# A new engine order, one semaphore per step, the attention product and the split maxima read from PSUM, and pair sums in a buffer of their own, in a fused attention and feed-forward kernel

## The reference

```python
def attention(q, k, v):                      # q = layernorm(x), k = v = ctx
    # (16, 256, 512) is read as 16 * 8 heads of (32, 512)
    qk = einsum('bdm,bdn->bmn', qh, kh) / sqrt(32)     # 512 x 512 scores per head
    return einsum('bmn,bcn->bcm', softmax(qk), vh)
def act_quant(x):                            # to 8 bit levels, one scale per token
    scale = 127 / clip(max(abs(x), axis=-1), 1e-5)
    return clip(round(x * scale), -128, 127) / scale
def weight_quant(w):                         # to -1, 0, 1, one scale for the matrix
    scale = 1 / clip(mean(abs(w)), 1e-5)
    return clip(round(w * scale), -1, 1) / scale
def bitlinear(x, w): return act_quant(x) @ weight_quant(w).T
x = x + attention(layernorm(x), ctx, ctx)
x = x + bitlinear(silu(bitlinear(layernorm(x), W1)), W2)   # W1 2048x512, W2 512x2048
```

## Time and profile before

| | |
|---|---|
| median of 3 executions | 919.39 us (917.77 to 921.04) |
| the profiled execution: its time, its span | 921.06 us, 919.0 us |
| busy PE, DVE | 791.9 us (86%), 789.7 us (86%) |
| busy ACT, POOL | 671.6 us (73%), 617.5 us (67%) |
| mean granted TensorE clock | 0.976 of full speed |

### The profile page before, as it was taken

The page is one execution under the profiler, slowest core; times in us unless marked ns, Lnnn a source line. Parts: engine busy times, 40 slices in busy tenths (PEclk is TensorE's granted clock), DMA queues, the critical chain, the costliest instruction groups (busy, mean ns, idle before and its releaser), DMA issues.

```text
span 919.0 us, 13936 instructions
## 1 busy us (share of the span) xinstructions
PE 791.9 (86%) x4580; PEld 292.9 (32%) x4580; DVE 789.7 (86%) x1624; ACT 671.6 (73%) x1089; POOL 617.5 (67%) x619
## 2 busy tenths in 40 slices
PE   1667799998999999999999999899999999989875
PEld 0322233333333333333333333333333333333222
DVE  1958799999999999999999999999999999998552
ACT  3485687877777777787777777787777778777753
POOL 4125578776777777777777777777777777875651
PEclk9977999999999999999999999999999999999997
DMA  8550333222333333312233333212233333120000
GB/s 264 156 158 18 70 81 70 61 63 63 71 81 81 82 81 70 82 47 65 63 81 81 82 81 81 70 50 67 60 79 81 81 82 81 47 58 25 24 12 23
DMA packets 49927, 68.28 MB, mean 74 GB/s; under 512 B 6336, under 2 KB 30912, under 8 KB 49344
## 3 DMA queue, kind: packets, MB, share of 16 engines
q1 hardware_dynamic: 49856, 67.39, 29.2%
HBM read 33.55 MB, written 8.39 MB: 46 GB/s over the span
## 4 chain that ended last, share of the span: by engine, by line
PE 51%; DVE 35%; issue 7%; POOL 3%; ACT 2%; DMA 1%; SPq 0%; POOLq 0%; ACTq 0%; DVEq 0%
PE bank_b L918 12%; DVE mx L703 11%; PE pv L887 9%; PE mxp L877 8%; PE st L867 7%; DVE hmx L782 6%; DVE late L777 6%; PE bank_b L956 4%; PE bank_a L956 3%; PE bank_a L908 3%; DVE cparts L713 2%; PE dn L898 1%; PE bank_a L926 1%; POOL late L492 1%; DVE sm L756 1%
## 5 line engine op out<-in xcount | busy, mean ns | idle before, releaser
L465 POOL TENSOR_TENSOR probs<-probs 128x512 f32<-128x512 f32 x256 | 332.8, 1317 | 138.5 <-PE pv L887 125.2
L703 DVE TENSOR_REDUCE mx<-mxp 128x1 f32<-128x512 f32 x512 | 338.1, 680 | 60.8 <-PE mxp L877 58.9
L546 ACT ACTIVATE probs<-st,sm 128x512 f32<-128x512 f32 x512 | 343.1, 686 | 53.0 <-PE st L867 49.8
L877 PE MATMUL mxp<-ks,qs 96*128 96x512 f16 x512 | 201.5, 395 | 56.8 <-DVE mx L703 24.9
L867 PE MATMUL st<-qs,ks 98*128 98x512 f16 x512 | 197.9, 388 | 5.3 <-DMA qs<-crow 3.1
L887 PE MATMUL pv<-probs,vt 128*32 128x512 f32 x1024 | 142.7, 630 | 0.0
L918 PE MATMUL bank_b<-w2t,late 128*128 128x512 f16 x512 | 134.7, 388 | 2.6 <-ACT late L578 2.6
L867 PEld LDWEIGHTS st<-qs,ks 98*128 98x128 f16 x512 | 50.1, 98 | 145.5 <-ACT probs L546 63.4
L877 PEld LDWEIGHTS mxp<-ks,qs 96*128 96x128 f16 x512 | 53.4, 105 | 132.1 <-DVE mx L703 65.2
L782 DVE TENSOR_REDUCE hmx<-late 128x1 f32<-128x512 f32 x128 | 84.6, 681 | 2.2
L609 ACT ACTIVATE late<-bank_a,sm 128x512 f32<-128x512 f32 x64 | 44.0, 688 | 50.4 <-PE bank_a L956 50.4
(11 more groups left out here) (92 smaller groups left out, 1024.9 us busy)
## 6 DMA issues: line engine op xcount, KB each, us to landing
xs<-x SPq DMA_DIRECT2D x32, 256.0 KB, 4.0
cs<-ctx SPq DMA_DIRECT2D x32, 256.0 KB, 4.1
ks<-kh SPq DMA_DIRECT2D x64, 128.0 KB, 3.4
qs<-qh SPq DMA_DIRECT2D x64, 128.0 KB, 3.7
xr<-x SPq DMA_DIRECT2D x32, 256.0 KB, 4.0
out<-late SPq DMA_DIRECT2D x32, 256.0 KB, 2.0
probs<-w SPq DMA_DIRECT2D x4, 1024.0 KB, 9.0
ks<-kl SPq DMA_DIRECT2D x32, 128.0 KB, 3.2
```

The costliest lines, as they stand in the source:

```text
L465: pool.tensor_tensor(probs[:, 2 * pair, h, :], probs[:, 2 * pair, h, :], probs[:, 2 * pair + 1, h, :], ALU.add).then_inc(sum_done, 1)
L546: act.activation(probs[:, c, h, :], st[u % 2][:, :], ACT.Exp, scale=sm1[:, r, ESC:ESC + 1]).then_inc(exp_done, 1)
L703: dve.reduce_max(mx[:, slot.ring(off), NC * h + c:NC * h + c + 1], mxp[m % 2][:, :], axis=AX.X).then_inc(max_done, 1)
L877: pe.matmul(mxp[m % 2][:, :], qs[0:3 * DH, r, h, c * P:(c + 1) * P], ks[0:3 * DH, r, h, :], start=True, stop=True).then_inc(mx_done, 1)
```

## The change

```diff
-    values=[6, 10, 15, 18],
-    sums=[6, 7, 8, 9, 14, 15, 16, 17],
-    denominators=[12, 19],
-    pv_evac=[18],
+    values=[16, 18, 19, 19],
+    sums=[2, 4, 5, 5, 7, 7, 7, 9],
+    denominators=[16, 18],
...
-    abs=[-18, -17, -16, -15, -2, -2, 2, 4],
-    ones=[-20],
-    sum=[-12, 5],
-    quantise=[-12, -11, -9, -9, 7, 9, 11, 15],
-    groups=[-10, -9, -7, -7, -6, -5, -4, -3, 9, 10, 12, 13, 15, 16, 18, 19],
+    abs=[-25, -23, -17, -16, -15, -9, -6, -2],
+    sum=[-14, 1],
+    quantise=[-14, -12, -11, -4, 2, 5, 9, 15],
+    groups=[-13, -12, -12, -7, -4, -3, -2, -1, 5, 8, 11, 13, 15, 17, 21, 23],
...
-                    wait_alone(pool, pv_done, slot, NC, off, 2 * pair + 1, passed)
+                    wait(pool, dn_done, slot, 2, off - 1, pair + 1)
                 wait(pool, exp_done, slot, UNITS, off, TH * (2 * pair + 1) + h + 1)
-                pool.tensor_tensor(probs[:, 2 * pair, h, :], probs[:, 2 * pair, h, :], probs[:, 2 * pair + 1, h, :],
+                pool.tensor_tensor(sums[:, pair, h, :], probs[:, 2 * pair, h, :], probs[:, 2 * pair + 1, h, :],
                                    ALU.add).then_inc(sum_done, 1)
...
-                if u % (2 * TH) == 0:
-
-                    wait(act, dn_done, slot, 2, -1, c // 2 + 1)
+                if h == 0:
+                    wait(act, pv_done, slot, NC, -1, c + 1)
+                wait(act, sum_done, slot, 2 * TH, -1, TH * (c // 2) + h + 1)
...
-                act.copy(pvs[:, slot.ring(off) % 2, :], pv[:, :]).then_inc(pv_evac, 1)
...
-                act.copy(crow[:, slot.ring(off) % 2, :], bank_a[0:2 * UNITS, 0:P // 2].bitcast(f16)).then_inc(ct_evac, 1)
+                act.copy(crow[:, slot.ring(off) % 2, 0, :], bank_a[0:UNITS, 0:P]).then_inc(ct_evac, 1)
...
+            dve.memset(ks[3 * DH:P, :, :, :], -1.0).then_inc(minus_ones, 1)
...
-                dve.tensor_copy(cparts[:, r, 0, :], mx[:, r, :]).then_inc(cpart_done, 1)
...
-                dve.tensor_tensor(cparts[:, r, 1, :], mx[:, r, :], cparts[:, r, 0, :], ALU.subtract).then_inc(cpart_done, 1)
+                dve.tensor_tensor(crow[:, k, 1, :], bank_a[0:UNITS, 0:P], crow[:, k, 0, :], ALU.subtract).then_inc(ct_low, 1)
...
-                dve.tensor_tensor(att[:, k, :], pvs[:, k, :], rden[:, :], ALU.mult).then_inc(token_scales, 1)
+                dve.tensor_tensor(att[:, k, :], pv[:, :], rden[:, :], ALU.mult).then_inc(attended, 1)
```

More of the change, by code:

```diff
@@ L50 @@
+    maxima=[-22, -21, -20, -20, -19, -18, -17, -15, -13, -12, -12, -10, -9, -9, -8, -7],
     vt=[-7],
-    vt_evac=[-7],
-    cparts=[-6],
+    vt_evac=[-8],
     ct=[-4],
     ct_evac=[-5],
-    values=[6, 10, 15, 18],
-    sums=[6, 7, 8, 9, 14, 15, 16, 17],
-    denominators=[12, 19],
-    pv_evac=[18],
-    invert=[20],
+    ct_low=[-4],
+    values=[16, 18, 19, 19],
+    sums=[2, 4, 5, 5, 7, 7, 7, 9],
+    denominators=[16, 18],
+    invert=[19],
     attend=[22],
-    residual=[23],
+    residual=[14],
@@ L82 @@
-    key_scale_b=[-28],
-    moments=[-32],
+    rstd2=[18],
+    xn2=[19],
+    absmax2=[25],
+    scale2=[25],
+    quantise=[20],
+    xqt=[27],
+    xqt_evac=[26],
+    first=[28, 29, 30, 31],
+    tanh=[28, 29, 31, 31],
+    gate=[28, 29, 32, 32],
+    hidden_max=[30, 32, 33, 34],
+    hidden_scale=[34],
+    hidden_quantise=[27, 28],
+    ht=[36, 39],
+    ht_evac=[36, 39],
+    second=[38, 39, 41, 42],
+    finish=[41],
+    max_read=[-21, -21, -21, -20, -19, -18, -16, -14, -11, -10, -10, -10, -8, -8, -7, -6],
@@ L103 @@
-    quantise=[-12, -11, -9, -9, 7, 9, 11, 15],
-    groups=[-10, -9, -7, -7, -6, -5, -4, -3, 9, 10, 12, 13, 15, 16, 18, 19],
-)
-ORDER = {'pool': ['key_rsqrt', 'xn', 'quantise', 'hidden_quantise', 'residual', 'ql', 'finish', 'rstd2', 'rstd',
-          'xn2', 'sums'],
- 'act': ['kh', 'vt_evac', 'tanh', 'ct_evac', 'qh', 'pv_evac', 'ht_evac', 'rescale', 'key_squares', 'xqt_evac',
-         'quantise_act'],
- 'dve': ['max_read', 'key_scale_b', 'cparts', 'norm2', 'cparts_low', 'aggregate', 'hidden_scale',
-         'hidden_scale_b', 'attend', 'hidden_scale_c', 'norm2b', 'absmax2', 'invert_b', 'key_scale',
-         'invert_c', 'invert', 'gate', 'hidden_max', 'moments2', 'hidden_scale_d', 'scale2', 'kl', 'scale2_b',
-         'moments', 'stats_x'],
- 'pe': ['xqt', 'key_norm', 'maxima', 'ct', 'values', 'vt', 'first', 'ht', 'second', 'denominators']}
+    abs=[-25, -23, -17, -16, -15, -9, -6, -2],
@@ new lines @@
+    sum=[-14, 1],
+    quantise=[-14, -12, -11, -4, 2, 5, 9, 15],
+    groups=[-13, -12, -12, -7, -4, -3, -2, -1, 5, 8, 11, 13, 15, 17, 21, 23],
+)
+ORDER = {'pool': ['residual', 'ql', 'sums', 'key_rsqrt', 'xn', 'xn2', 'hidden_quantise', 'rstd2', 'finish',
+          'quantise', 'rstd'],
+ 'act': ['tanh', 'qh', 'rescale', 'kh', 'key_squares', 'xqt_evac', 'vt_evac', 'quantise_act', 'ht_evac',
+          'ct_evac'],
+ 'dve': ['norm2', 'hidden_max', 'key_scale_b', 'moments', 'invert', 'norm2b', 'hidden_scale_c', 'ct_low',
+          'moments2', 'kl', 'scale2_b', 'hidden_scale_d', 'attend', 'hidden_scale_b', 'invert_c',
+          'max_read', 'absmax2', 'key_scale', 'invert_b', 'stats_x', 'gate', 'scale2', 'hidden_scale',
+          'aggregate'],
+ 'pe': ['vt', 'ht', 'maxima', 'key_norm', 'xqt', 'ct', 'first', 'second', 'values', 'denominators']}
@@ L153, in wait @@
     value = slot.at(per_tile, off, more)
[L155 to L156 removed]
+    if value > 0:
         engine.wait_ge(sem, value)
[L160 to L165 removed]
 def build(nc, x, ctx_in, w1, w2, out):
@@ L335, in load @@
                 r = slot.ring(off)
[L337 removed]
+                wait(sp, vt_evac, slot, 1, off - RING, 1)
                 t = slot.at(1, off, 0)
@@ L524, in run @@
                                 steps[name](slot, off, *number)
-                    for at, step, *which in weights:
-                        if not slot.looped and at == UNITS * slot.b + u:
-                            step(*which)
             for b in range(-3, TILES + 2):
-                run(Slot(0, b, False))
+                run(Slot(b))
         @block.scalar
@@ L893, in denominators @@
                 if pair == 0:
-                    if not slot.looped and slot.b + off == 0:
+                    if slot.b + off == 0:
                         pe.wait_ge(w_evac, WG)
-                    wait(pe, token_scales, slot, T_HIDDEN, off - 1, D_SPREAD)
+                    wait(pe, dn_spread, slot, 1, off - 1, 1)
                 for h in range(TH):
-                    last = pe.matmul(dn[DH * h:DH * (h + 1), :], ones[:, 0:DH], probs[:, 2 * pair, h, :],
+                    last = pe.matmul(dn[DH * h:DH * (h + 1), :], ones[:, 0:DH], sums[:, pair, h, :],
                                      start=(pair == 0), stop=(pair == 1), skip_group_check=True)
```

366 lines of the change are left out of this document (177 added, 189 removed).

## The result

The changed kernel takes 814.11 us in the median (813.79 to 816.58, four executions), the kernel before 919.30 (917.77 to 921.04): a ratio of 0.886 (95% interval 0.885 to 0.888). The profiled execution took 816.58, its span is 814.8, against 919.0.

A forecast was written before the change was run, and what follows sets the result against it. No engine was full: PE was to be the fullest, with 22.5 us of own work and some waits a lap. Span 113.6 + 28 x 23.6 + 74.1 = 848.5, so 850 us forecast, range 826 to 893.

The forecast's parts named there:

- The lap, 23.6: One middle lap: 22.5 us of PE's own work, 0.9 of stalls and 0.2 for `kl`; bounds 22.8 and 24.6.
- Stalls, 0.9: PE's waits in a lap of the new order, walked queue by queue: together 0.7 to 0.9 us.
- `kl`, 0.2: DVE, end of the lap: `kl` beside POOL's work costs 0 to 0.8 us more, partly covered; 0.2 added.
- `attend` at 0.69: DVE: `attend` with one operand in PSUM takes 0.69 us, saving 1.0 a lap; bounds 0.67 and 1.76.
- `ct_low` at 0.3: DVE: the new step `ct_low`, with one operand in PSUM, takes 0.3 us, at worst 1.10.
- The second transfer of the maxima at nothing: SP: a second DMA adds a 0.70 us issue but costs the lap nothing; upper bound 1.3 at every S0.
- Semaphores at nothing, `sums` for what it waits only: One semaphore per step costs nothing; on POOL, buffer `sums` changes only what the adds wait for.
- Beginning, 8 earlier: Up to the first `ht0`: 8 us earlier, at 113.6; bounds 0 and 14 us.
- End, 3 off: After the last full lap: 1.5 us off each of two laps without reads, 74.1; bounds 72 and 79.
- PE full: Rival, chance 0.08: stalls absorbed and the beginning gains its most; 22.8 us a lap, 820 to 829.
- Half of the waits come back: Rival, chance 0.22: in-order waits on four engines return; 24.4 to 25.4 us a lap, 870 to 899.
- the fourth rival: Slower, chance 0.06: a loop from POOL's sums through `denominators1`, `invert` and hidden scale to `ht0`; 26.4 a lap, 932.

The follow-up runs named there:

- one run more: `denominators0` one unit later, against the changed kernel with `kl` moved ahead of `hidden_max`: 822.05 us, against 814.94 without it; laps of 22.80.
- two of the edits above: Changed kernel with one edit each: W2's last four transposes earlier, 830.45 us; the -1 memset back on POOL, 831.48 us.
- old order and old parts: Kernel before with only new semaphores, buffer `sums`, SP's order, memset on DVE and `key_scale_b` form: 890.98 us, ratio 0.967.
- both old parts together: Changed kernel with ACT's copy of `pv` (`attend` from SBUF) and the 16-bit maxima split before the transpose put back: 886.73 us, ratio 0.961.
- one of them: Changed kernel with only ACT's copy of `pv` put back, 856.97 us; with only the old maxima split put back, 869.17 us.
- the new parts make of the old order: Changed kernel with the old order tables, keeping `attend` from PSUM and the new maxima split: 1019.13 us, ratio 1.106.
- the same edit: New maxima split: in the old order with `attend` from SBUF, 884.18 us; old split put back in the changed kernel, 869.17 us.

## Why the prediction was wrong

Taken step by step:

- **The lap, 23.6: wrong, 22.64 measured.** The step that failed is its first term, the 22.5 us of PE's own work. I read 22.5 in the old order and kept it for the new one, although the walk itself put `values` and `denominators` side by side. Adding up PE's spacings from start to start, the six groups take 6.63 a lap before and 5.94 after, and all of PE's own work 22.5 and 21.8. The experiments put 0.24 on one run more; three runs fewer make 0.7. Over 28 laps that is 20 of the 27 us missed in the middle; the stalls give 4 more and `kl` 3. The term's "0.1 at each change between 32 and 16 bit operands" was also wrong in kind: the rows tie the cost to the 32 columns of weights.
- **Stalls, 0.9: near.** About 0.76 remain in a lap of 22.56 (22.56 - 21.8). The chain names two of them as reads of maxima; the first is `maxima11` behind read 9, as walked.
- **`kl`, 0.2: too much, and right in kind.** POOL and `kl` do hold each other off, and its longest is 1852 ns, but in the changed kernel POOL is the one held in most laps (median 744). The long laps add 22.64 - 22.56 = 0.08. That it did not cost 16 us was luck that I did not price: two of the edits above, both of steps at the beginning, fell on the other side in most laps and paid it.
- **`attend` at 0.69: right,** 676 ns. That is also what the Trainium skill, page "SBUF — State Buffer", section "Who interferes with whom", says of an instruction with only one input in SBUF; the trace agrees, 671 to 692 over all 32. But the value of reading `pv` in place, 0.95 a lap, is the wait for ACT's copy that it saves in this order, not the lock: from SBUF `attend` took 693, and in the old order the buffer `sums` alone freed it from POOL. My account of the gain was right in size and wrong in cause.
- **`ct_low` at 0.3: right,** 270 ns. DVE's lap of 21.9 was 21.17, 0.7 too high; it no longer was the question.
- **The second transfer of the maxima at nothing: right.** No DMA stands at S0 in the chain or in the waits.
- **Semaphores at nothing, `sums` for what it waits only: too low.** With old order and old parts the kernel still gains 0.78 a lap. `sums` explains 0.33 of it. Whether the sum suffered by it is not shown, since I walked the new order as a whole and no run has it without these edits.
- **Beginning, 8 earlier: near,** 10.5. S0 of tile 0 did not move (52.78 against 52.89), so all of it lies in the two laps after it; PE is busy 24.01 instead of 19.94 between 60 and 90 us, at 0.86 of its clock instead of 0.73. The memset delayed the first key scale from 6.4 to 9.4, the bound I gave, and that cost nothing.
- **End, 3 off: too little,** 7.3. The last three laps are shorter by about 2.2, 3.3 and 1.5. PE is busy 20.20 of 21.30 and 16.82 of 18.90 us in the first two; in the third it is busy 9.04 of 16.60, so PE does not set that one, but its clock is 1.00 where it was 0.83 before.

The rival "PE full" asked for 820 to 829 and had 0.08. It came closest and is still above the result, for the same reason: it too stood on 22.5. Its 22.8 a lap, also my lower bound, let the waits go but held the work fixed. The range failed there and nowhere else: with 21.8 in the sum, the forecast lap is 22.9 and the time 830, and the range reaches the result.

"Half of the waits come back" asked for laps of 24.4 to 25.4. In the new order that is what both old parts together give (24.95 in the mean) and nearly what one of them gives (23.89 and 24.36). A slower kernel is what the new parts make of the old order, by another wait than the loop that the fourth rival named. The change works only as a whole: `attend` from PSUM asks for an order in which `values0` comes long after it, and in the new order, with the last `values` just ahead of `attend`, a copy between them costs 0.95 at the place where it was tried.

Not settled: 0.45 of the 0.78 a lap that old order and old parts gain lies with the semaphores, SP's order, the moved memset or `key_scale_b`, which were not tried apart.

## What to carry to other kernels

Add up PE's own work anew for each new order: matmuls with 32 columns of weights that stand together are cheaper than the same ones spread out, and a floor read from the old order is not a floor. Then price a part in the order that it will live in; the same edit was worth 0.23 in one order and about 1.2 in another, and reading `pv` in place cost 4.5 a lap in one (24.7 to 29.2, part of it by the lower clock) and gained 0.95 in the other. When laps jump between two lengths, look for two instructions that start together on DVE and POOL, and move one of them into a gap of the other.
